# A fused conv-MoE, attention and MoE kernel on one core: layer norm applied in two wide operations per half, q and k stacked by head triples, maxima begun four slots earlier

## The reference, cut to what matters

```
x = x + moe_a(group_norm(x))            # 8 experts, top 2, hidden 384, gelu
t = t + attention(layer_norm(t))        # 6 heads of 16, causal; on the whole
                                        # token rows of one image
t = t + moe_c(layer_norm(t))            # 4 experts, top 2, hidden 384, gelu

def _ln_t(v, eps=1e-05):
    m = jnp.mean(v, axis=-1, keepdims=True)
    s = jnp.var(v, axis=-1, keepdims=True)
    return (v - m) / jnp.sqrt(s + eps)

att = jnp.einsum('bhqd,bhkd->bhqk', q, k) * (1.0 / np.sqrt(hd))
att = jax.nn.softmax(jnp.where(causal, att, -jnp.inf), axis=-1)
y = jnp.einsum('bhqk,bhkd->bhqd', att, v)
```

## Time and profile before

| what | value |
|---|---|
| median of three runs | 1520.64 us (1518.58 to 1526.09) |
| the profiled execution | 1521.14 us, span 1519.3 us |
| PE busy | 1309.2 us (86%) |
| ACT busy | 946.4 us (62%) |
| DVE busy | 904.2 us (60%) |
| POOL busy | 785.3 us (52%) |
| granted clock of PE, mean | 0.913 |

### The profile page before, as it was taken

The page is one execution under the profiler, slowest core; times in us unless marked ns, Lnnn a source line. Parts: engine busy times, 40 slices in busy tenths (PEclk is TensorE's granted clock), DMA queues, the critical chain, the costliest instruction groups (busy, mean ns, idle before and its releaser), DMA issues.

```text
span 1519.3 us, 32843 instructions
## 1 busy us (share of the span) xinstructions
PE 1309.2 (86%) x12573; PEld 757.5 (50%) x12573; DVE 904.2 (60%) x2662; ACT 946.4 (62%) x1880; POOL 785.3 (52%) x782
## 2 busy tenths in 40 slices
PE   4788878889898899898998898988998898968877
PEld 1554542466535564365635565365643666232355
DVE  4866583378717784287734777167852876165353
ACT  2566547566685567656686666755677566704745
POOL 4775541557536474366725575364744566201546
PEclk9897998999999899999999899998999999956988
DMA  5000200400031000400003000310003000120100
GB/s 110 12 2 15 50 1 12 75 2 2 13 60 26 2 2 23 74 2 2 3 22 75 2 2 13 62 25 1 2 23 65 1 2 2 39 47 1 24 12 12
DMA packets 37390, 34.76 MB, mean 23 GB/s; under 512 B 26091, under 2 KB 28012, under 8 KB 37234
## 3 DMA queue, kind: packets, MB, share of 16 engines
q1 hardware_dynamic: 20594, 26.37, 9.0%
q10 hardware_dynamic: 16640, 6.29, 1.6%
HBM read 22.62 MB, written 9.63 MB: 21 GB/s over the span
## 4 chain that ended last, share of the span: by engine, by line
PE 55%; DVE 23%; DMA 7%; issue 4%; DVEq 3%; ACT 3%; POOL 3%; SPq 2%; POOLq 0%; ACTq 0%
PE ps_y L636 20%; PE ps_u L636 18%; PE ps_r L636 9%; PE ps_m L636 6%; DVE mpart L1156 5%; DVE xn L1138 4%; DMA qk_dram<-qk_l 3%; DVE acc L1097 3%; DMA ks<-qk_dram 3%; POOL hidl L615 2%; DVE yt L1288 2%; PE ps_m L655 1%; ACT hidh L928 1%; DVEq L1140 1%; SPq L505 1%
## 5 line engine op out<-in xcount | busy, mean ns | idle before, releaser
L615 POOL TENSOR_TENSOR hidl<-hid,hidh 128x512 f16<-128x512 f32 x576 | 673.5, 1184 | 389.8 <-ACT hidh L928 383.9
L927 ACT ACTIVATE hid<-ps_u 128x512 f32<-128x512 f32 x576 | 344.2, 598 | 402.3 <-PE ps_u L636 373.9
L636 PEld LDWEIGHTS ps_y<-w2s,hidh 128*128 128x128 f16 x4608 | 289.7, 101 | 166.3 <-issue 38.5
L1156 DVE TENSOR_REDUCE mpart<-ps_r 128x1 f32<-128x512 f32 (+2 forms) x576 | 297.3, 549 | 102.1 <-PE ps_r L636 91.0
L636 PE MATMUL ps_y<-w2s,hidh 128*128 128x96 f16 x4608 | 336.5, 212 | 7.2 <-DVE acc L1097 7.2
L928 ACT ACTIVATE hidh<-ps_u 128x512 f16<-128x512 f32 x576 | 341.2, 592 | 0.0
L636 PE MATMUL ps_r<-ks,qs 96*128 96x512 f16 (+2 forms) x576 | 203.6, 369 | 88.6 <-DVE mpart L1156 51.5
L636 PE MATMUL ps_y<-w2s,hidl 128*128 128x96 f16 x2304 | 233.2, 212 | 4.8 <-POOL hidl L615 3.9
L587 POOL TENSOR_SCALAR_AFFINE_SELECT probs<-probs 128x384 f32<-128x384 f32 x128 | 66.7, 523 | 306.5 <-ACT probs L959 306.4
L636 PE MATMUL ps_u<-xah,w1h 97*128 97x512 f16 x408 | 169.8, 416 | 22.2 <-ACT hidh L928 17.3
L959 ACT ACTIVATE probs<-ps_r 128x512 f32<-128x512 f32 (+3 forms) x352 | 152.2, 506 | 45.1 <-PE ps_r L636 45.0
(11 more groups left out here) (183 smaller groups left out, 1487.3 us busy)
## 6 DMA issues: line engine op xcount, KB each, us to landing
rb<-rsum_dram SPq DMA_DIRECT2D x24, 256.0 KB, 4.3
qs<-qk_dram SPq DMA_DIRECT2D x24, 192.0 KB, 4.7
ks<-qk_dram SPq DMA_DIRECT2D x24, 192.0 KB, 4.9
xin<-in_x_dram ACTq DMA_DIRECT2D x8, 384.0 KB, 4.3
qk_dram<-qk_h SPq DMA_DIRECT2D x16, 192.0 KB, 2.9
qk_dram<-qk_l SPq DMA_DIRECT2D x16, 192.0 KB, 3.5
out_dram<-xo ACTq DMA_DIRECT2D x8, 384.0 KB, 2.9
w_raw<-in_L_conv_W_dram SPq DMA_DIRECT2D x8, 288.0 KB, 5.0
```

The lines of the kernel that those rows point to most:

```text
L615: g.tensor_tensor(hidl[:, grp.k % HB, j, :], hid[:, j, :], hidh[:, grp.k % HB, j, :], ALU.subtract).then_inc(hl_ready, 1)
L636: return nc.tensor.matmul(dst, lhsT, rhs, start=start, stop=stop, skip_group_check=True)
L927: a.activation(hid[:, j, :], bank[:], ACT.Gelu, scale=1.0 / WS)
L1156: v.tensor_reduce(mpart[:, h, i, part:part + 1], ps_r[k % 3][:, 0:w], AX, ALU.max).then_inc(mx_free, 1)
```

## The change

Four edits, made together.

1. `ln_apply`: the four `tensor_scalar` operations on 96 columns each (subtract the mean, multiply by the reciprocal deviation) become two `tensor_tensor` operations on 384 columns with broadcast second operands, one that subtracts and, behind a drain, one that multiplies in place.
2. q and k are first both written to DRAM (`keep_qk`). Then the reads into `qs` and `ks` are issued by head triples: six reads of half the size for heads 0 to 2, which wait only for the first half of the current softmax's scores, and six for heads 3 to 5, which wait for all of them. Units 0 to 35 of the maxima wait for the first triple, unit 36 for the second.
3. The tables: the 56 maxima of phase A are spread over slots 3 to 63 in place of 8 to 63; `x2_turn`, `logits_c`, `exp_c` and the last `route_c` move by one slot, `x_turn` from slots 37 and 39 to 39 and 42.
4. The scaling by -1/256 is folded into the split that follows, so one DVE operation and a drain go from `maxima`.

```
-TO_C = [(27, "ln2_apply", 0), (28, "ln2_apply", 1), (30, "x2_turn", 0), (32, "x2_turn", 1), (34, "logits_c", 0),
-        (36, "exp_c", 0)]
+TO_C = [(27, "ln2_apply", 0), (28, "ln2_apply", 1), (31, "x2_turn", 0), (33, "x2_turn", 1), (35, "logits_c", 0),
+        (37, "exp_c", 0)]
-GN = [(37, "x_turn", 0), (39, "x_turn", 1), ...
+GN = [(39, "x_turn", 0), (42, "x_turn", 1), ...
-                   *maxima_at(8, SLOTS_A - 1, 0, MAX_A)),
+                   *maxima_at(3, SLOTS_A - 1, 0, MAX_A)),

-                if s == 0:
-                    wait(sp, s_full, b.value(SU, 0))
-                wait(sp, qk_out, b.value(64, 32 * (s + 1)))
-                dst, parts = ((qs, (0, 1, 0)), (ks, (0, 0, 1)))[s]
-                for n, part in enumerate(parts):
-                    sp.dma_start(dst[HD * n:HD * (n + 1), :, :],
-                                 qk_dram[part, s].rearrange("(h d) t -> d h t", h=H)).then_inc(qk_stacked, 16)
+            def stack_qk(t, b):
+                wait(sp, s_full, b.value(SU, (t - 1) * half))
+                wait(sp, qk_out, b.value(64, 64))
+                heads = slice(TR * t, TR * (t + 1))
+                for s, (dst, parts) in enumerate(((qs, (0, 1, 0)), (ks, (0, 0, 1)))):
+                    for n, part in enumerate(parts):
+                        sp.dma_start(dst[HD * n:HD * (n + 1), heads, :],
+                                     qk_dram[part, s, heads.start * HD:heads.stop * HD, :]
+                                     .rearrange("(h d) t -> d h t", h=TR)).then_inc(qk_stacked[t], 16)

                 if k == 0:
-                    pe.wait_ge(qk_stacked, b.value(16 * QK_DMAS, 16 * QK_DMAS))
+                    pe.wait_ge(qk_stacked[0], b.value(16 * QK_DMAS, 16 * QK_DMAS))
                     wait(pe, p_ready, b.value(SU, 0))
+                if k == MAXU // 2:
+                    pe.wait_ge(qk_stacked[1], b.value(16 * QK_DMAS, 16 * QK_DMAS))

-                for t in range(TC * half, TC * (half + 1)):
-                    v.tensor_scalar(dst[:, t, :], src[:, t, :], mv[:, t, 0:1], rstd[:, t:t + 1],
-                                    ALU.subtract, ALU.mult)
+                ts = slice(TC * half, TC * (half + 1))
+                v.tensor_tensor(dst[:, ts, :], src[:, ts, :], mv[:, ts, 0:1].to_broadcast([P, TC, D]), ALU.subtract)
+                dve.drain()
+                v.tensor_tensor(dst[:, ts, :], dst[:, ts, :], rstd[:, ts].unsqueeze(2).to_broadcast([P, TC, D]), ALU.mult)

-                v.tensor_scalar(used, used, -1.0 / MS, None, ALU.mult).then_inc(mneg_ready, 1)
...
-                split(mth[:], mtl[:], ps_m[0:H * TT, 0:P], 1.0).then_inc(m_free, 1)
+                split(mth[:], mtl[:], ps_m[0:H * TT, 0:P], -1.0 / MS).then_inc(m_free, 1)
```

More of the change, by code:

```diff
@@ L359, in build @@
         mpart = sb("mpart", [P, H, TT, 2])
-        mneg = sb("mneg", [P, P])
+        mtop = sb("mtop", [P, P])
         mth = sb("mth", [H * TT, P], F16)
@@ L436, in build @@
         acc_ready = sem("acc_ready")
-        qk_split, qk_out, qk_stacked = sem("qk_split"), sem("qk_out"), sem("qk_stacked")
+        qk_split, qk_out = sem("qk_split"), sem("qk_out")
+        qk_stacked = [sem(f"qk_stacked{t}") for t in range(2)]
         v_ready = sem("v_ready")
         hi_ready = sem("hi_ready")
-        mneg_ready, m_split, m_stacked = sem("mneg_ready"), sem("m_split"), sem("m_stacked")
+        mtop_ready, m_split, m_stacked = sem("mtop_ready"), sem("m_split"), sem("m_stacked")
         yt_ready, sums_in, rsum_ready = sem("yt_ready"), sem("sums_in"), sem("rsum_ready")
@@ L446, in build @@
         QK_DMAS = 2 * 3
+        half = SU // 2
         x_d = x.rearrange("b (t q) w c -> b (q w) t c", t=TT)
@@ L530, in chore @@
                 if name == "qk" and k % NC == NC - 1:
-                    stack_qk(k // NC, b)
+                    keep_qk(k // NC, b)
+                    if k // NC == 1:
+                        for t in range(2):
+                            stack_qk(t, b)
                 if name == "maxima":
@@ L562, in _ @@
             pool.drain()
-            for tile, value in ((identb, 0.0), (mask_q, 0.0), (mpart, NEG), (mneg, 0.0)):
+            for tile, value in ((identb, 0.0), (mask_q, 0.0), (mpart, NEG), (mtop, 0.0)):
                 g.memset(tile[:], value)
@@ L1160, in maxima @@
                 dve.drain()
-                used = mneg[:, 0:H * TT]
-                v.tensor_reduce(used.rearrange("p (h i) -> p h i", h=H), mpart[:], AX, ALU.max)
-                dve.drain()
-                v.tensor_scalar(used, used, -1.0 / MS, None, ALU.mult).then_inc(mneg_ready, 1)
+                used = mtop[:, 0:H * TT]
+                v.tensor_reduce(used.rearrange("p (h i) -> p h i", h=H), mpart[:], AX, ALU.max).then_inc(mtop_ready, 1)
                 wait(dve, m_stacked, b.value(32, 0))
                 shared()
-                split(mth[:], mtl[:], ps_m[0:H * TT, 0:P], 1.0).then_inc(m_free, 1)
+                split(mth[:], mtl[:], ps_m[0:H * TT, 0:P], -1.0 / MS).then_inc(m_free, 1)
                 dve.drain().then_inc(m_split, 1)
```

10 lines of the change are left out of this document (5 added, 5 removed).

## The result

The changed kernel takes 1417.88 us, the median of four runs (1416.04 to 1420.12), beside 1519.61 us for the kernel before (four runs, 1512.69 to 1526.09). The ratio is 0.9332, with a 95% interval of 0.9288 to 0.9376: 102 us faster, where 69 were forecast.

What follows compares the result with a forecast made beforehand. PE was taken as the bound, with gain from its idle time and the low clock behind it. Terms of -10 - 26 - 27 - 2 - 4 = -69 took 1521 to about 1452 us; own range 1436 to 1472, of all 1424 to 1490.

Steps and rivals of the forecast that it cites:

- moved chores: Moved table entries: the 1.76 us wait before `x_turn` goes, -1.2 us an image; last `route_c` put at 0.
- the 36: Low clock behind PE's waits at `ln2_apply`, `ln1_apply` and `x_turn`: up to 6 us an image, left out of the sum.
- 8.6 us of clock: Slow PE work behind five of the six steady waits for `ks`, 1.7 us each, expected to go.
- Rival 2: Clock comes back too, as waits shrink and PE stays at 2.4 GHz: -96 us, about 1425; chance 0.15.
- Stacking: Reads by head triples end waits for `ks`: -26 us in six steady images, -10 in iteration 8, 0 in iteration 1.
- rival 1: DVE becomes the bound: PE waits for the reciprocal and reductions, layer norm gives nothing; -28 us, about 1493; chance 0.17.
- Rival 3: Half reads do not overlap and hold back the sums and reciprocal, so the kernel is slower: 1583 us; chance 0.03.
- Layer norm: Wide operations shorten PE's waits: -2.0 us an image at `ln2_apply`, -1.3 at `ln1_apply`, -2 in filling and draining iterations.
- The 27: Six steady images at -4.5 us each, from `ln2_apply`, `ln1_apply` and the wait before `x_turn`.
- The fold: In `maxima`, one DVE operation and a drain less, once per attention image: 8 x 0.5, -4 us.

Runs made afterwards that it cites:

- spread memsets: Changed kernel with 14 DVE memsets per steady image, one ahead of the reduction at each of 14 maxima units; 1455.96 us, ratio 0.9600.
- one stop of 14: Changed kernel with one DVE delay of 14 memsets per steady image, at maxima unit 48; 1510.75 us, ratio 0.9958.
- two stops of 4: Changed kernel with two DVE delays per steady image of four memsets each; 1449.07 us, ratio 0.9551.
- two stops of 7: Changed kernel with two DVE delays per steady image, seven memsets each, ahead of maxima units 12 and 48; 1524.97 us, ratio 1.0061.
- two stops of 10: Changed kernel with two DVE delays per steady image, ten memsets each, ahead of maxima units 12 and 48; 1553.33 us, ratio 1.0228.

## Why the prediction was wrong in size, step by step

**The step that failed** is in the part on the moved chores: "The lower bound is the clock: behind these three waits it is low as well (...), which I put at up to 6 us an image, -36. I leave it out of the sum, since waits near 2 us may remain." The sum counted 8.6 us of clock in the six images; they gave 50.4. With the 36 in it the sum would have been 1521 - 105 = 1416, the measured time. In the kernel before, PE was busy for 62.6 us of low clock at these three places; half of that, 31 us, is an estimate of what it cost. What remained there were waits of 1.42 us, of 0.87 and 1.49, and none, and behind 28 of 30 waits the clock was full. Rival 2 had the mechanism, with a chance of 0.15, and took two thirds of the 36. The range followed it no further than 1424, and so missed.

Why it was a bad choice: the three waits had been cut by 2.0, 1.3 and 1.2 us in the same sum, from 2.21, 2.43 and 1.76, which leaves 0.2 to 1.1 us each. By its own terms no wait near 2 us remained.

**Place by place**, in the six images, in us. Idle time is PE's, before less after; clock is half of PE's busy time at the low clock of the kernel before, an estimate.

| place | idle, forecast | idle, measured | clock, forecast | clock, estimate |
|---|---|---|---|---|
| reads of `ks`, less new waits in slots 4 to 8 | 17.6 | 17.3 | 8.6 | 9.9 |
| `ln2_apply`, `x2_turn` | 12.0 | 5.9 | left out | 12.8 |
| `ln1_apply`, `gn_apply` | 7.8 | -2.6 | left out | 11.7 |
| `x_turn` | 7.2 | 2.5 | left out | 6.8 |
| last `route_c` | 0 | 10.2 | 0 | 9.9 |
| folded scale | 3 | 3.8 | | |
| other places | | 1.3 | | 5.1 |
| all six images | 47.6 | 38.4 | 8.6 | 56.2 (50.4 measured) |

That the sum with the 36 in it meets the measured time is in part luck: at three places the idle time was put too high, and `route_c`, put at nothing, made up for it in both columns.

**Stacking.** The mechanism was right. Waits for `ks` are gone in all six images and in iteration 8, and 4.15 us are left in iteration 1 (4.72 before), as foreseen. The reciprocal runs 8.4 us behind the second triple's issue, 8 were forecast; rival 1 needed more than 10. PE waits there for a bank in three images (1.61, 0.42 and 0.59 us), 2.6 in all, near the 2.4 us that I counted. Iteration 8 gave 11.2 us for 10, of it 9.5 idle time. Rival 3 did not come: six half reads in front of the sums held the reciprocal no later than counted.

**Layer norm.** The 64 new operations take 0.56 to 1.51 us and 71.9 us in all, between the 60 and 80 of the forecast, so a half takes 2.25 us in the mean where it took 2.67. At `ln1_apply` PE's waits grew shorter one by one but not in sum: in four of six images 0.87, 1.48 and 1.14 us stand where one of 2.43 or 2.53 us stood, alone or with one of 0.45 behind it, and over the six images the sum rose from 16.0 to 18.7 us. What was won there is clock. DVE's groups by form after (busy, mean ns) answer to the earlier trace rows:

```profile
L1151 DVE TENSOR_TENSOR xn<-xn,rstd 128x384 f32<-128x384 f32 x32 | 40.4, 1261 | 2.4
...
L1149 DVE TENSOR_TENSOR xn<-x,mv 128x384 f32<-128x384 f32 x32 | 31.5, 986 | 9.3 <-POOL rstd L605 8.1
```

The Trainium skill ("VectorE: DVE Perf Modes", the tier table) would give fp32 `tensor_scalar` two elements a cycle and `tensor_tensor` one, so that the edit is worth nothing. Alone it gained 1.33% (0.7 to 2.0), and 28 us within the change. So the rule doesn't decide here: no half of the old form reached the page's rate for it, an estimated 0.83 us (the shortest took 1.05, where the prediction says 1.10), and what PE waits for is how soon the next reduction starts. My own term has a right size for a wrong reason. It was 22 us of idle time (3.3 us in six images and 2 us); alone the edit took 5.2 us of idle time and 15.7 us of busy time, and undone it cost 4.0 and 21.4.

**The moved chores.** This term was most under its size: 1.2 us an image, 7 in all, where alone they gave 25 us and undoing them cost 32, of it 11 to 12 idle time. The wait before `x_turn` went (9.5 to 0.7 us), but a wait of 1.23 us for ACT's gelu came in its place, so that 2.5 us of 7.2 were won. The last `route_c` I put at 0: PE's wait of 2.72 us behind it, for which the prediction has no row, is gone, and 0.68 us for its gates is left (2.07 in the last image):

```profile
876.66 0.39 PE L636 MATMUL ps_r<-ks,qs 96*128 96x512 f16 x1 [2.72 <-DVE mpart L1156]
```

**Idle time alone**: 38.4 us of it went in the six images, where the terms hold 47.6 (20.0 - 2.4 + 27 + 3 for the fold). Only the reads and the fold have the right size by themselves. The 27 for the layer norm and the moves came to 16, 10 of them at a place that the prediction put at 0.

**The fold.** 4 us forecast; the wait fell by 4.3 us.

**Left open.** When a short wait is followed by the low clock is not settled. The same product behind the same wait of 1.48 us at `ln1_apply` had a full clock behind it in five of six images of the changed kernel, in four with the spread memsets, in three with the one stop of 14, in two with two stops of 4 and in none with two stops of 7. The wait of 2.84 us in the kernel with the spread memsets had 0.50, 1.00, 0.69, 1.00, 0.69 and 0.50 in its six images. Nor does the length decide. In the kernel with two stops of 10, waits of 1.99 to 2.38 us at `ln2_apply` had a full clock behind them in all six images, and those of 1.48 us at `ln1_apply` had the low clock in all six. And with the moved chores alone the wait at `ln1_apply` kept its 2.43 us, but the clock behind it was full in four images, where the kernel before had it low in all six. That earlier waits in the same image matter is a guess from these counts, and no run parted it from where in time the wait falls. Whether the fold alone is worth more than its 4.4 us is not known either.

## What to carry to other kernels

Where one engine is the bound and its granted clock falls behind its waits, price each wait twice, as idle time and as the slow products behind it: here a wait of 3 us and more cost some 3 to 4 us on top, whether it was 4 or 12 us long, and removing or splitting many waits of 2 to 3 us paid more than their idle time said. Below 3 us a wait's length alone did not tell whether the low clock would follow. If the terms of a sum already shorten the waits that much, the clock behind them belongs into it, or the sum contradicts itself. A delay put in on purpose, at one size and at a larger one, tells the two prices apart. And a term is put at 0 only after the timeline has been read for the waits near its place.
